# A graph attention layer and a normalised adjacency product: its first stage written out, with the mask work five tiles behind

## What is computed

```python
# layer 1: graph attention, H = 16 heads of DH = 32
seq = (x @ W_seq).reshape(N, H, DH)
score1 = jnp.einsum('nhd,d->hn', seq, a1)
score2 = jnp.einsum('nhd,d->hn', seq, a2)
scores = leaky_relu(score1[:, :, None] + score2[:, None, :], 0.2)
scores = scores + (1.0 - adj)[None, :, :] * -65500.0
attn = softmax(scores, axis=-1)
hidden = einsum('hij,jhd->ihd', attn, seq).reshape(N, D_IN) @ W_out + b_out
x = layernorm(x + elu(hidden))
# layer 2: B = (adj + adj.T) / 2 + I, scaled by its row sums d
#   y = adj @ (d**-0.5 * B * d**-0.5) @ x
x = layernorm(x + y)
```

## Time and profile before

| what | value |
| --- | --- |
| median of three runs | 851.83 us |
| the profiled execution | 855.83 us |
| its span, from first to last instruction | 853.9 us |
| mean granted TensorE clock over the span | 0.968 |
| prologue, to the first attention product | 140.0 us |

### The profile page before, as it was taken

The page is one execution under the profiler, slowest core; times in us unless marked ns, Lnnn a source line. Parts: engine busy times, 40 slices in busy tenths (PEclk is TensorE's granted clock), DMA queues, the critical chain, the costliest instruction groups (busy, mean ns, idle before and its releaser), DMA issues.

```text
span 853.9 us, 24026 instructions
## 1 busy us (share of the span) xinstructions
PE 765.0 (90%) x10017; PEld 565.9 (66%) x10017; DVE 664.9 (78%) x995; ACT 479.0 (56%) x473; POOL 168.8 (20%) x159
## 2 busy tenths in 40 slices
PE   1999944989999999999999999798879999999996
PEld 0666634989999999999999999343324444444442
DVE  5677856999899999999999996789966666344444
ACT  2465626988788888998888885366431111100000
POOL 1000002233333322333333213044300000000000
PEclk9999986998999999999999999899969999999999
DMA  6566544111011111101111120421434454001110
GB/s 235 180 210 226 184 143 178 52 53 51 5 51 51 52 51 52 52 12 43 51 51 52 51 64 28 112 62 49 115 82 133 138 156 113 1 37 38 45 43 37
DMA packets 46466, 71.30 MB, mean 83 GB/s; under 512 B 1952, under 2 KB 34720, under 8 KB 42144
## 3 DMA queue, kind: packets, MB, share of 16 engines
q1 hardware_dynamic: 46384, 70.03, 24.6%
HBM read 61.37 MB, written 8.65 MB: 82 GB/s over the span
## 4 chain that ended last, share of the span: by engine, by line
issue 39%; PE 39%; DVE 12%; POOL 4%; ACT 3%; DMA 1%; DVEq 1%; POOLq 0%; SPq 0%; ACTq 0%
PE bank L577 18%; PE bank L580 10%; PE bank L502 7%; DVE RZ L997 5%; DVE RG L1008 3%; POOL RZ L469 2%; ACT RZ L747 2%; DVE RG L1012 2%; PE bank L521 2%; PE bank L509 2%; POOL rstd L465 1%; PE bank L494 1%; DMA AV<-in_L_gnn_a_dram 1%; DVE W L883 1%; DVE WA L885 1%
## 5 line engine op out<-in xcount | busy, mean ns | idle before, releaser
L577 PE MATMUL bank<-RP,RG 128*128 128x132 f16 x4096 | 372.1, 220 | 46.0 <-DVE RG L1008 23.9
L577 PEld LDWEIGHTS bank<-RP,RG 128*128 128x128 fp8e4 x4096 | 369.3, 98 | 47.9 <-issue 47.9
L580 PE MATMUL bank<-RP,MT 128*128 128x66 f16 x4096 | 371.7, 194 | 0.0
L580 PEld LDWEIGHTS bank<-RP,MT 128*128 128x128 fp8e4 x4096 | 368.3, 96 | 0.0
L747 ACT ACTIVATE RZ<-RZ,KB 128x2048 int8<-128x2048 f32 x160 | 307.1, 2024 | 0.3 <-DVE RG L1008 0.3
L1008 DVE TENSOR_TENSOR RG<-RZ,MT 128x512 int32<-128x512 int32 x160 | 136.9, 856 | 0.5 <-ACT RZ L747 0.5
L997 DVE TENSOR_SCALAR RZ<-RZ,KB 128x2048 int8<-128x2048 f32 x96 | 135.3, 1410 | 0.3 <-DVE DSL L1050 0.3
L654 PE MATMUL bank<-RG,RP 128*128 128x512 f16 x512 | 116.6, 388 | 8.7 <-DVE RG L1144 7.3
L654 PE MATMUL bank<-RZ,MT 128*128 128x512 f16 x512 | 110.7, 379 | 0.0
L654 PEld LDWEIGHTS bank<-RG,RP 128*128 128x128 bf16 x512 | 49.8, 99 | 75.6 <-DVE RG L1144 11.3
L654 PEld LDWEIGHTS bank<-RZ,MT 128*128 128x128 fp8e4 x512 | 50.1, 98 | 60.4
(11 more groups left out here) (117 smaller groups left out, 724.1 us busy)
## 6 DMA issues: line engine op xcount, KB each, us to landing
RG<-in_adj_dram SPq DMA_DIRECT2D x16, 1024.0 KB, 4.9
RZ<-s_rows_dram SPq DMA_DIRECT2D x16, 1024.0 KB, 4.7
RP<-in_adj_dram SPq DMA_DIRECT2D x16, 1024.0 KB, 5.8
RZ<-in_x_dram SPq DMA_DIRECT2D x32, 256.0 KB, 2.6
seq_copy_dram<-SEQ SPq DMA_DIRECT2D x1, 4224.0 KB, 17.3
out_dram<-W SPq DMA_DIRECT2D x16, 256.0 KB, 2.0
RZ<-in_L_gnn_W_seq_dram SPq DMA_DIRECT2D x1, 1024.0 KB, 5.2
RZ<-in_L_gnn_W_out_dram SPq DMA_DIRECT2D x1, 1024.0 KB, 5.3
```

What stands on the lines that cost most here:

```text
L577: mm(pb[bank][:, c:c + 4 * DV], G8[:, s, i * P:(i + 1) * P], PN[:, u, j, 0:4, :].rearrange("p c d -> p (c d)"), start=(j == 0 and i % IB = ...
L580: last = mm(pb[bank][:, c + 2 * DV:c + 4 * DV], MT8[:, j, i * P:(i + 1) * P], PN[:, u, j, 4:6, :].rearrange("p c d -> p (c d)"), start=Fal ...
```

## The change

The tile loops of the prologue are written out in Python, and the parts of a tile are taken apart. The variable n counts the steps of TensorE, ScalarE and VectorE alike.

- x comes in four loads of 1 MB. x(0) is issued ahead of W_seq; adj has four buffers.
- In step n TensorE transposes x tile n+2 and multiplies tile n with W_seq. The transposed x of four tiles is kept together, and the product with WA is made once for four tiles with WA as the stationary operand, so that the scores come out as 32 rows (L507). They are turned back into columns by 16 small transposes (L515).
- The mask of tile n-5 (LEAD = 5) is transposed in step n, behind the product of tile n. ScalarE casts adj tile n-4, and moves the first half of mask n-6, in step n. VectorE makes mask n-5 and moves the second half of mask n-6.
- The column sums of adj are 16 products per tile with a single column of ones (L528), and the DVE additions (L907) are gone.
- The maxima over the partitions go through a TensorE transpose, a DVE reduction, and a product with the identity. Both partition_all_reduce are gone, and each partition computes the flag of the general path by itself.
- The table chain stands in steps 16 to 20, between the last masks. WA is made by VectorE in steps 0 to 3, behind its first two moves of transposed x.

```diff
@@ sync @@
+            load_x(0)
             sp.dma_start(WS, w_seq.rearrange("(k p) d -> p k d", p=P)).then_inc(wseq_in, 16)
...
+            load_x(1)
+            load_adj(0)
+            load_x(2)
+            load_adj(1)
+            load_x(3)
+            for t in range(2, NT):
+                if t >= NA:
+                    sp.wait_ge(adjb_done, t - NA + 1)
+                load_adj(t)
@@ gpsimd @@
-            gp.wait_ge(red_done, 2)
-            gp.partition_all_reduce(VC[:, :], red[:, :, :].rearrange("p e h -> p (e h)"), P, RMAX).then_inc(allred, 1)
...
-            own.mark(gp.partition_all_reduce(WID[:, 3:4], WID[:, 2:3], P, RMAX))
@@ tensor @@
+            def score_product(g):
+                if g == 0:
                     pe.wait_ge(wa_done, 1)
+                else:
+                    pe.wait_ge(s_sb, g)
                 for k in range(KC):
+                    last = mm(pb[4][0:2 * H, :], WA[:, k, :], xT[:, g % 2, k, :], start=(k == 0), stop=(k == KC - 1))
                 last.then_inc(s_ps, 1)
...
+            def mask_tiles(t):
+                u = t % 2
                 pe.wait_ge(mask_done, t + 1)
                 for half, (ps, evacuated, bank) in enumerate(((mtA_ps, mtA_sb, 5), (mtB_ps, mtB_sb, 6))):
+                    if t >= 1:
                         pe.wait_ge(evacuated, t)
...
+                for j in range(NT):
+                    last = mm(pb[7][:, j:j + 1], adj_b[:, u, j * P:(j + 1) * P], ones[:, 0:1],
+                              start=(t == 0 and j == 0), stop=(t == NT - 1), skip_group_check=True)
+                last.then_inc(col_ps, 1)
...
+            for n in range(NT + LEAD):
+                if n + 2 < NT:
+                    x_transpose(n + 2)
+                if n < NT:
+                    seq_product(n)
+                if n % GT == 1 and GT < n < NT:
+                    score_product(n // GT - 1)
+                if n == NT - 1:
+                    score_product(NT // GT - 1)
+                    pe.wait_ge(xT_sb, NT)
+                    for g in range(NT // GT - 1):
+                        score_columns(g)
+                if n == NT:
+                    score_columns(NT // GT - 1)
+                if n >= LEAD:
+                    mask_tiles(n - LEAD)
...
@@ scalar @@
+            def cast_adj(t):
+                u = t % 2
+                sc.wait_ge(adj_in[t % NA], (t // NA) * 16 + 16)
+                if t >= 2:
                     sc.wait_ge(mask_done, t - 1)
+                    sc.wait_ge(col_ps, t - 1)
...
+            for n in range(NT + LEAD + 1):
+                if n < NT:
+                    move_seq(n)
+                if 0 <= n - LEAD + 1 < NT:
+                    cast_adj(n - LEAD + 1)
+                if n % GT == 1 and GT < n < NT:
+                    move_scores(n // GT - 1)
+                if n == NT - 1:
+                    move_scores(NT // GT - 1)
+                if n == NT + 2:
+                    exponentials()
+                if n >= LEAD + 1:
+                    move_mask(n - LEAD - 1)
@@ vector @@
+            ve.wait_ge(consts, 5)
+            move_xT(0)
+            move_xT(1)
             ve.wait_ge(wseq_in, 16)
             ve.wait_ge(a_in, 32)
+            for n in range(NT + LEAD + 1):
+                if n < 4:
+                    if n % 2 == 0:
+                        scores_of(n // 2)
+                    else:
+                        scores_sum(n // 2)
...
+                if n + 2 < NT:
+                    move_xT(n + 2)
+                if n == NT + 1:
+                    top_rows()
+                if 0 <= n - LEAD < NT:
+                    mask_tile(n - LEAD)
+                if 1 <= n <= NT:
+                    max_seq(n - 1)
+                if n == NT:
+                    score_tables()
+                if n == NT + 2:
+                    exponents()
+                    scales()
+                if n == NT + 4:
+                    scale_tables()
+                if n >= LEAD + 1:
+                    move_mask(n - LEAD - 1)
```

More of the change, by code:

```diff
@@ L125, in gat_then_normalised_adjacency @@
         S1, S2, EE, FF, AA, BBT = (TAB[:, i] for i in range(6))
-        VMT = T[:, :, 0, 0:H]
-        VC = sb("VC", [P, 2 * H], f32)
-        VM, C2 = VC[:, 0:H], VC[:, H:2 * H]
+        VC = sb("VC", [P, 3 * H], f32)
+        VM, C2, N2 = (VC[:, i * H:(i + 1) * H] for i in range(3))
         RV = sb("RV", [P, H], f32)
-        red = sb("red", [P, 2, H], f32)
+        red = sb("red", [P, 3 * H], f32)
+        TOPS = sb("TOPS", [3 * H, 1], f32)
+        TOPB = sb("TOPB", [3 * H, P], f32)
         WID = sb("WID", [P, 4], f32)
@@ L298, in _ @@
                 sp.dma_start(AV[:, i, :], a.rearrange("(o d) -> o d", o=1).broadcast_to([P, DH])).then_inc(a_in, 16)
[L300 to L320, removed]
+            load_x(1)
[7 more added lines that the diff above has]
+                load_adj(t)
+            sp.wait_ge(s_sb, NT // GT)
+            sp.dma_start(s1_rows[:, :], sT[0:H, :]).then_inc(s1_stored, 16)
             sp.wait_ge(s1_stored, 16)
@@ L921, in _ @@
-            ve.wait_ge(consts, 6)
-            move_xT(0, 0, True)
-            prologue_tile(0, 0, fresh=True, more_fresh=True)
-            prologue_tile(1, 1, fresh=True)
-            with ve.Fori(1, NT // 2 - 1) as p:
-                own.enter(p, 1, 2)
-                for u in range(2):
-                    prologue_tile(p * 2 + u, u)
-                own.leave(NT // 2 - 1)
-            prologue_tile(NT - 2, 0)
-            prologue_tile(NT - 1, 1, more=False)
-            ve.wait_ge(vm_done, NT)
@@ L945, in _ @@
-            own.mark(V.tensor_tensor(EE, S2, c2b, ALU.subtract))
-            own.mark(V.tensor_tensor(AA, S1, c2b, ALU.add))
-            own.wait(ve)
-            own.mark(V.tensor_scalar(BBT, AA, 0.0, None, ALU.max))
-            own.wait(ve)
-            own.mark(V.tensor_scalar(AA, AA, 0.0, None, ALU.min))
-            own.wait(ve)
-            V.tensor_scalar(S2, S2, -1.0, None, ALU.mult).then_inc(texp_in, 1)
-            own.mark(V.tensor_copy(SEQ[:, :, :, DH], VM[:, :].unsqueeze(1).broadcast_to([P, NT, H])))
@@ new lines, in top_rows, with exponents @@
+            def top_rows():
+                ve.wait_ge(red_ps, 1)
+                own.mark(V.tensor_reduce(TOPS[:, :], pb[1][0:3 * H, 0:P], AX.X, ALU.max))
+                own.wait(ve)
+                V.tensor_copy(TOPB[:, :], TOPS[:, :].broadcast_to([3 * H, P])).then_inc(top_sb, 1)
+            def exponents():
+                ve.wait_ge(top_ps, 1)
+                own.mark(V.tensor_copy(VC[:, :], pb[2][:, 0:3 * H]))
+                own.wait(ve)
+                c2b = C2.unsqueeze(2).broadcast_to([P, H, NT])
+                own.mark(V.scalar_tensor_tensor(EE, S2, -1.0, c2b, ALU.mult, ALU.subtract))
+                own.mark(V.tensor_tensor(AA, S1, c2b, ALU.add))
+                own.mark(V.tensor_scalar(VM, VM, 1e-30, None, ALU.max))
+                own.wait(ve)
+                own.mark(V.tensor_scalar(BBT, AA, 0.0, None, ALU.max))
+                own.wait(ve)
+                V.tensor_scalar(AA, AA, 0.0, None, ALU.min).then_inc(texp_in, 1)
@@ new lines, in scales, with scale_tables @@
+            def scales():
+                own.mark(V.tensor_copy(SEQ[:, :, :, DH], VM.unsqueeze(1).broadcast_to([P, NT, H])))
+                own.mark(V.reciprocal(RV[:, :], VM))
+                own.wait(ve)
+                own.mark(V.tensor_scalar(RV[:, :], RV[:, :], TOP * SPLIT, None, ALU.mult))
+                own.wait(ve)
+            def scale_tables():
+                rvb = RV[:, :].unsqueeze(2).broadcast_to([P, H, NT])
+                ve.wait_ge(texp_out, 1)
+                own.mark(V.tensor_tensor(EE, EE, rvb, ALU.mult))
+                own.mark(V.tensor_tensor(FF, FF, rvb, ALU.mult))
+                own.wait(ve)
+                V.memset(RD[:, :], 1.0).then_inc(tabs_done, 1)
```

260 lines of the change are left out of this document (110 added, 150 removed).

## The result

The changed kernel takes 890.35 us in the median of 4 runs (888.12 to 890.57), the kernel before 851.5 us in 4 runs on the same chip: a ratio of 1.0447 (95% interval 1.0423 to 1.047), 38.9 us slower. The forecast was 901 us. The profiled execution took 890.14 us (span 888.3) against 855.83 (853.9), so the two profiles are 34.3 us apart.

What follows compares the result with a forecast made beforehand. TensorE was taken to bound the prologue; a first attention product 28.7 us later plus 20.6 us of lost clock made 905.1 us for the profile, 901.1 for the median, range 878 to 914.

Steps and rivals of the forecast that it cites:

- The start: First product with W_seq starts at about 10.7 us against 18.57, a gain of 7.9 us, bounded by 5 and 10.
- The wait: Steps 6 to 15: after each product TensorE stands still 3.85 us for ScalarE's SEQ move, cast and mask move.
- The warm lap: Tile loop, one product to the next at full clock: 9.51 us in place of 5.76.
- the wait is hidden: Rival: mask move done before TensorE asks, 6.4 us per tile, the change wins at about 843 us; chance 0.05.
- The clock: Pauses of 3.85 us return TensorE to half clock, costing 20.6 us in loop and tail together.
- 2.2 us in eight of the nine laps (17.6): The loop's share of the half-clock cost, from 4.0 to 5.9 us at half clock per burst.
- The tail: Behind tile 15: last masks, exponentials and tables, first attention product at 168.7 us, 28.7 later than before, without clock cost.
- The code load: GpSimd's 11.57 us idle behind MODIFY_POOL_CONFIG was taken as all gone; bound: some 4.6 us stays.
- The sum: 28.7 + 20.6 = 49.3 us on the profiled 855.83 gives 905.1; less 4.0 for a median, 901.1 us.
- ring: Behind the last product, cast, mask move, masks and sums still follow in turn: 4.74 us per tile, masks 11 to 13.

Runs made afterwards that it cites:

- e3: Changed kernel plus 13 bf16 products with unread results ahead of TensorE's wait for the mask move: 878.06 us, ratio 1.0309.
- e2: Changed kernel with ScalarE's mask move placed between the move into SEQ and the cast: 856.83 us, ratio 1.0044.
- e1: Changed kernel with ScalarE's mask move first in its step instead of last: 842.32 us, ratio 0.9868.
- e9: Changed kernel with masks three tiles behind the products instead of five, ScalarE's order kept: 896.05 us, ratio 1.0527.
- e7: Changed kernel with ScalarE's mask move first and a lag of three tiles instead of five: 841.39 us, ratio 0.9872.
- e8: Changed kernel with ScalarE's mask move first and a lag of two tiles instead of five: 841.32 us, ratio 0.9858.
- e11: e8 with VectorE's half of the mask move also ahead of the maxima and score tables: 839.83 us, ratio 0.9861.
- e4: Changed kernel with one partition_all_reduce put back on GpSimd, its result unused: 894.17 us, ratio 1.0479.
- e5: Kernel before, with VectorE's first move of transposed x ahead of making WA: 852.09 us, ratio 0.9994.
- e10: Kernel before, with the SEQ copy and head 1's score-row load issued behind head 0's second tensor product: 846.63 us in one run.
- e6: Kernel before, with only the SEQ copy issued behind head 0's second tensor product: 851.3 us, ratio 0.9993.

## Why the forecast was right, and what in it was not

**The start: right.** The first product was put at 10.7 us and came at 10.63; W_seq landed at 9.68, forecast about 10. Product 0 took 5.45 us where I had taken 6.65, and steps are 3.87 us for 4.06, because the lead-in of a product row lies beside the row ahead of it. Tile 6 started at 40.71, not 43.1: 2.4 us less. The first product is a matter of the execution: it took 4.55 us (e3) to 6.08 (e2) with the same code, and 5.05 to 6.65 with the code of before. That it began at half clock is read from its weight loads, 0.86 us apart to 14.05 us and 0.43 from 14.63 on; PEclk reads 1.00 for all of it, in the profile before too, and doesn't show it.

**The wait: right, and shown.** The idle ahead of line 525 was put at 3.85 us, ended by line 700; it is 3.58. The warm lap (at full clock) was put at 9.51 us; it is 8.87 in e3 and 8.94 summed from the chain (3.45 + 3.57 + 1.05 + 0.38 + 0.49). Seven such laps, two with a score product (10.65) and the last two without x transposes (less 0.49 each) make 82.9 us for the forecast's 87.5. e1 takes the wait away by order alone, e9 keeps it at another lag. The rival "the wait is hidden" was right about its own case, partly by luck: it said 843 us, and e1 took 842.32, but e1's laps from tile 6 to 15 are 5.9 us in the mean for its 6.4, and its tail of 35.8 us is longer than the rival had room for.

**The clock: right in kind, mis-sized in the sum.** The term "2.2 us in eight of the nine laps (17.6)" failed. Tiles 6 to 15 took 94.1 us against 82.9 warm, which leaves 11.2 us, 1.2 to 1.4 per lap. I had taken 4.0 to 5.9 us at half from the earlier trace rows, but in this loop each stretch lasted 3.4 us, 1.7 us of work lost at most, and the eighth lies for the most part behind the start of tile 15. e3 agrees: its 84.4 us less the 1.9 that the filler adds are 82.5, 11.6 below the change. The Trainium skill (TensorE: Matmul & The Clock Gate, section "HAM oscillation — how this bites in real kernels") had the direction, half clock back in every tile, in a kernel with waits of about 3 to 5 us. The seven pauses of 3.58 us agree; the shorter ones of e2 lie outside its case.

**The tail: the number about right, its last step wrong.** From tile 15's start to the first attention product I had 38.1 + 3 of clock = 41.1 us; it was 42.3. Up to GpSimd's copy I had 30.1 and 3 of clock, and it was 33.4 (134.83 to 168.22). From there I had carried over 7.5 us from the kernel before, and it was 8.9: ScalarE's L737 waited for the last column sums and not for GpSimd's product. My sum had no term for masks 14 and 15 behind the last table product; in the change they are the last to end, while in e1, e7, e8, e9 and e11 L737 waits for GpSimd. The 3 us of clock have no run of their own.

**The code load: gone, as forecast, and worth less than it looked.** e4 puts it at 6.2 us of the prologue in the changed kernel; in the whole time it is at the edge of what can be told. The Trainium skill (GPSIMD Engine Reference, section Instruction dispatch) has about 6 us for such a first call; here 7.52 and 8.00 us were the shortest behind the first such load, and the earlier trace rows have 7.01 behind the second.

**The sum.** 905.1 us was forecast for the profile and 890.14 came, 15.0 less: tile 6 (2.4), the warm laps (4.6), the clock of the laps (6.4), against it the tail (1.2), and 2.7 us that lie behind the first attention product, where I had forecast no change. The 4.0 us taken off for the median belonged to one profiled execution of the kernel before; the one of the change stood at its median (890.14, 890.35). Taking them off brought the forecast nearer by luck. That is why the medians are 11 us from the forecast and the profiles 15.

## What to carry to other kernels

Where an engine's list is in order, ask of every wait on a freed buffer what stands ahead of the instruction that frees it: the move that frees must stand ahead of whatever needs the waiting engine's newest product, or two engines take turns (48 us here for one place in a list). A share of busy time, or a free 44% of ScalarE, says nothing on that. And an early start is worth only what the next need lets through (7.2 us at the first product, 1.2 at the second).

## What the runs showed that I had not expected

- The clock came back after 3.4 us in the loop of the change, eight times, where the earlier trace rows had shown over 4 us, and 6.8 us in e5.
- Of seven pauses of 1.69 us, one in each lap of 7.06 us, six left the granted clock at 1.00 and the last was followed by half clock (e2). In the change one of two pauses of 1.67 us was followed by half clock too, so the length of a pause alone doesn't decide.
- Useless products made a kernel faster by 12.3 us, of which 9.7 lie in the laps (e3).
- GpSimd's first instruction behind its first load of code came 7.5 to 11.6 us later (e4, e10, e6 and the kernel before: 7.52, 8.00, 9.78, 11.57). In the last three it is longer with more traffic in the DMA queues; e4, with the whole copy in them, is the shortest.
- With the masks five tiles behind and the wait in every ring, the masks ended behind the tables and held head 0 for 1.7 us (the change); with the wait gone, ScalarE waited for GpSimd's product instead (1.3 us in e1).
